# Decoder layer on one core: the PSUM bank of a score tile by its number in the whole walk, not within its pair of heads

## The reference, cut to what matters

```
q = concat([q_nope, rope(q_rope)]);  k = concat([k_nope, rope(k_rope)])
scores = einsum('blhd,bmhd->bhlm', q, k) / sqrt(DN + DR)
scores = where(tril, scores, -1e30)
attn = softmax(scores, axis=-1)
out = einsum('bhlm,bmhd->blhd', attn, v)
return out.reshape(B, L, H * DV) @ w_o
```

## Time and profile before

| | us |
|---|---|
| median of 3 runs | 1344.37 (1344.04 to 1345.14) |
| profiled execution, its own time | 1342.33 |
| its span, first to last instruction | 1340.50 |
| mean granted TensorE clock | 0.901 of full speed |
| attention walk, first to last score tile | about 165 to 928 |

### The profile page before, as it was taken

The page is one execution under the profiler, slowest core; times in us unless marked ns, Lnnn a source line. Parts: engine busy times, 40 slices in busy tenths (PEclk is TensorE's granted clock), DMA queues, the critical chain, the costliest instruction groups (busy, mean ns, idle before and its releaser), DMA issues.

```text
span 1340.5 us, 19020 instructions
## 1 busy us (share of the span) xinstructions
PE 1014.4 (76%) x6220; PEld 572.2 (43%) x6220; DVE 1043.0 (78%) x2856; ACT 678.5 (51%) x1451; POOL 273.0 (20%) x507
## 2 busy tenths in 40 slices
PE   1535488799989899989989999996834452547998
PEld 0323244445445445445445555553332331324564
DVE  5589677877887877887877888887189888886886
ACT  1539656656656656656656665654024221533443
POOL 1000112212212212212212221221021313122111
PEclk9759899899999989999989999999975776767999
DMA  9100022332332342322343333345271010000001
GB/s 358 69 1 1 1 50 49 68 58 50 68 61 50 67 115 52 67 58 50 68 112 58 60 69 64 91 97 154 71 220 47 17 32 0 0 1 8 35 38 48
DMA packets 200433, 86.59 MB, mean 65 GB/s; under 512 B 174600, under 2 KB 185864, under 8 KB 199824
## 3 DMA queue, kind: packets, MB, share of 16 engines
q1 hardware_dynamic: 200336, 85.38, 26.4%
HBM read 36.06 MB, written 7.34 MB: 32 GB/s over the span
## 4 chain that ended last, share of the span: by engine, by line
DVE 39%; PE 30%; ACT 12%; issue 10%; POOL 8%; DMA 1%; SPq 1%; DVEq 0%; ACTq 0%; POOLq 0%
PE bank L1765 5%; PE bank L889 4%; DVE arena L1471 4%; ACT arena L1204 4%; DVE arena L1447 4%; PE bank L1663 4%; DVE arena L1464 4%; POOL arena L1029 3%; ACT arena L1192 3%; POOL arena L1035 3%; PE bank L904 2%; DVE arena L648 2%; PE bank L1715 2%; DVE arena L644 2%; DVE arena L607 2%
## 5 line engine op out<-in xcount | busy, mean ns | idle before, releaser
L1174 ACT ACTIVATE arena<-bank,arena,scal 128x128 f32<-128x128 f32 (+3 forms) x256 | 158.1, 617 | 256.3 <-POOL arena L1024 253.8
L1765 PE MATMUL bank<-arena 128*128 128x512 f16 x768 | 186.0, 388 | 17.1 <-DVE arena L1477 12.8
L1447 DVE TENSOR_REDUCE arena<-bank 128x1 f32<-128x128 f32 (+3 forms) x256 | 124.0, 484 | 42.2 <-PE bank L1738 42.1
L1024 POOL TENSOR_TENSOR arena<-arena,scal 128x1 f32<-128x1 f32 x256 | 48.5, 190 | 529.2 <-DVE arena L1447 529.2
L1471 DVE SCALAR_TENSOR_TENSOR arena<-arena 128x128 f16<-128x128 f32 (+3 forms) x256 | 142.0, 555 | 9.1
L1464 DVE TENSOR_SCALAR arena<-arena 128x128 f16<-128x128 f32 (+3 forms) x256 | 140.9, 551 | 4.9
L1715 PE MATMUL bank<-arena 128*128 128x512 f16 x576 | 140.1, 390 | 0.0
L1750 PE MATMUL bank<-arena 128*128 128x512 f16 (+3 forms) x768 | 118.2, 305 | 19.6 <-DMA arena<-arena 19.4
L1765 PEld LDWEIGHTS bank<-arena 128*128 128x128 f16 x768 | 72.9, 99 | 99.9 <-DVE arena L1477 14.8
L1733 PE MATMUL bank<-arena 128*128 128x128 f16 (+3 forms) x256 | 77.5, 303 | 33.0 <-ACT arena L1174 25.2
L1482 DVE TENSOR_TENSOR arena<-bank,arena 128x512 f16<-128x512 f32 x64 | 43.9, 686 | 70.4 <-ACT arena L1183 70.4
(11 more groups left out here) (211 smaller groups left out, 2091.7 us busy)
## 6 DMA issues: line engine op xcount, KB each, us to landing
arena<-in_L_attn_w_qb SPq DMA_DIRECT2D x1, 4608.0 KB, 20.7
arena<-in_x SPq DMA_DIRECT2D x4, 1024.0 KB, 5.6
arena<-in_L_attn_w_o SPq DMA_DIRECT2D x1, 4096.0 KB, 31.0
arena<-arena SPq DMA_TRANSPOSE x256, 2.8
arena<-in_fside_BxS2xS SPq DMA_DIRECT2D x4, 1024.0 KB, 5.5
arena<-in_L_ffn_w SPq DMA_DIRECT2D x8, 512.0 KB, 7.8
out<-arena SPq DMA_DIRECT2D x16, 256.0 KB, 2.0
arena<-in_x SPq DMA_DIRECT2D x12, 256.0 KB, 3.1
```

Source lines behind the costliest of these rows:

```text
L1174: act.activation(pf(k), banks[S_BANKS[g % 3]][:, 0:n], ACT.Exp, bias=NB[:, k:k + 1], scale=sc_exp, accum_out=SUM[:, k:k + 1]).then_inc(s_e ...
L1447: dve.tensor_reduce(NEGM[:, (g & 3):(g & 3) + 1], banks[S_BANKS[g % 3]][:, 0:n], AX.X, ALU.max, negate=True).then_inc(s_max, 1)
L1765: last = pe.matmul(banks[Y_BANK][:, :], ot(gp, a, k, (q & 3) * P, P), wo(b, gp * GH + k), start=(k == 0 and n == 0), stop=(k == GH - 1 and ...
```

## The change

A tile's bank becomes S_BANKS[G % 3], on TensorE, VectorE and ScalarE alike, so that the rotation goes on from pair to pair. TensorE's wait becomes s_exp >= G - 2 for each tile from the fourth on: every tile takes the bank of the tile three before. For tile 0 of a pair that is the old tile 5, for tile 1 the old tile 6, for tile 2 the old tile 7. Nothing else is changed.

```diff
@@ exps (ScalarE)
-                act.activation(pf(k), banks[S_BANKS[g % 3]][:, 0:n], ACT.Exp, bias=NB[:, k:k + 1], scale=sc_exp,
+                act.activation(pf(k), banks[S_BANKS[G % 3]][:, 0:n], ACT.Exp, bias=NB[:, k:k + 1], scale=sc_exp,
                                accum_out=SUM[:, k:k + 1]).then_inc(s_exp, 1)
@@ row_max (VectorE)
-                dve.tensor_reduce(NEGM[:, (g & 3):(g & 3) + 1], banks[S_BANKS[g % 3]][:, 0:n], AX.X, ALU.max,
+                dve.tensor_reduce(NEGM[:, (g & 3):(g & 3) + 1], banks[S_BANKS[G % 3]][:, 0:n], AX.X, ALU.max,
                                   negate=True).then_inc(s_max, 1)
@@ scores (TensorE)
-                h, k, bp = g >> 2, g & 3, (i >> 3) & 1
-                n, bank = (k + 1) * P, banks[S_BANKS[g % 3]]
+                h, k, bp, G = g >> 2, g & 3, (i >> 3) & 1, 8 * i + g
+                n, bank = (k + 1) * P, banks[S_BANKS[G % 3]]
...
-                if not (i == 0 and g < 3):
-                    pe.wait_ge(s_exp, 8 * i + (g - 2 if g >= 3 else (-1, 0, -2)[g]))
+                if G >= 3:
+                    pe.wait_ge(s_exp, G - 2)
```

## The result

The changed kernel is slower: median 1349.05 us (8 runs, 1347.06 to 1351.47) against 1345.16 us of the kernel before (8 runs), ratio 1.0029 [1.0017, 1.0041]. That is +3.9 us, where +2.1 was forecast; it lies 0.25 us above the range. A second measurement, made beside the last experiments, gave 1349.06 (5 runs) against 1343.98 (21 runs), ratio 1.0042 [1.0028, 1.0055]. The profiled execution took 1347.66 us (span 1345.8), 5.3 us more than that of before.

A forecast was written before the change was run, and what follows sets the result against it. No engine was seen as full; VectorE's gapless queue mostly set the pace. Clock cost +2.4 and chain gain -0.3 gave +2.1 us, from 1342.33 to 1344.4 us, range 1343.3 to 1348.8.

The forecast's parts named there:

- Its mechanism and its sign: Merged TensorE idling in pairs 2 and 4 lowers the clock on chain work; slower by 2.1 us in sum.
- The gain on the chain: Tile 1 of pairs 25, 27 and 29 starts earlier, worth 0.1 us each on the chain, 0.3 us together.
- Tile 0: At a pair's start it still waits for qn_lo; idling shrinks about 0.06 us, bounds 0 and 0.12.
- Most of the 25.2 us are gone: TensorE's score matmul waits for the exp, 25.2 us in 20 waits, would mostly vanish from the profile.
- Tile 2: Its tighter wait, for the exp of old tile 7, costs 0; 2.4 us are left in pair 19.
- The clock in pairs 2 and 4: Clock falls in 4.6 us of merged idling, slowing prep_t to tile 3: 1.18 us each, bounds 0 and 4.76.
- its rival on the slow side: Slow clock in pairs 2 and 4 covers all of prep_mm: +4 to +6 us, 1348.4 to 1350.4; chance 0.27.
- the all-of-prep_mm case: In pairs 2 and 4 prep_mm goes from 3.10 to 6.2 us, each pair losing 2 to 3 us; chance 0.27.
- The steady blocks: In steady odd pairs TensorE gets 0.2 to 0.5 us ahead; clock cost taken as 0, bounds 0 and 1.2 us.

The follow-up runs named there:

- 4, 9 or 14 matmuls in pairs 2 and 4 alone: Changed kernel with that many unread matmuls before prep_t in pairs 2 and 4: 1345.14 and 1344.61 us with 4, 1342.55 with 9, 1342.74 with 14.
- filling: Kernel before, with 5 unread matmuls in TensorE's idle time before prep_t (even pairs 6 to 22) and before project (pairs 4 to 20): 1338.81 us.
- the two with old waits: Changed kernel with old waits at tiles 0 and 1 of each pair, 1345.54 us; or at tile 1 of pairs 2 and 4 only, 1344.80 us.

## Why the prediction was wrong

Its mechanism and its sign were right; the sizes of two terms were not.

- **The gain on the chain** (0.3 us): right in kind and near in size. The exp's step at pair 25 left the chain, VectorE's queue took its place, and pairs 25 to 30 gave 0.54 us.
- **Tile 0** keeps its wait, 2.30 us at 211.20 against 2.45 before, held by qn_lo: right, with 0.15 us gone where the bound was 0.12. "Most of the 25.2 us are gone" was wrong: 14.7 stay under the exp's name. They are not waits for it. At the start of pair 2 qn_lo ended at 211.14 (210.45 + 0.69), tile 0 began at 211.20, and the exp of the old tile 6, which it no longer waits for, ended at 211.21 (211.02 + 0.19):

```profile
210.45 0.69 DVE L1482 TENSOR_TENSOR arena<-bank,arena 128x512 f16<-128x512 f32 x1 [2.56 <-ACT arena L1183]
211.02 0.19 ACT L1174 ACTIVATION_READ_ACCUMULATOR arena<-bank,arena,scal 128x1 f32 x1
```

- **Tile 2** costs nothing: right, as the two traces of the changed kernel show.
- **The clock in pairs 2 and 4** (1.18 us each): this is the first step that failed. It was read from a block in which the clock fell 0.8 us after prep_t had begun. Here it fell before prep_t, and the slow stretch was 6.8 us, not 3.4, so prep_t and tile 2 paid too: 1.61 and 1.59 us in one trace, 1.94 and 1.75 in the other. The prediction had this as its rival on the slow side and gave the all-of-prep_mm case 2 to 3 us a pair; the truth lies between, and the slow clock covered prep_t and tile 2 but not all of prep_mm. Against that rival stood "such a stretch lasted 3.4 us here". The trace of the kernel before had a longer one, in pair 4, which the prediction took as pair 2's twin: 0.50 from 262.38 to 269.21 us, 6.8 us, begun in the idling before tile 1. It shows in nope_mm, which took 4.01 us there and 2.11 at the full clock:

```profile
264.22 0.39 PE L1733 MATMUL bank<-arena 128*128 128x256 f16 x1 [1.91 <-ACT arena L1174]
...
265.36 4.01 PE L1715 MATMUL bank<-arena 128*128 128x512 f16 x9
```

- **The steady blocks** (taken as 0, bounds 0 and 1.2 us): the second. Both traces of the changed kernel have falls in three blocks (at 373, 575 and 677 us in the first) where that of before has two (470 and 672): from pair 8 to pair 21 they take 2.4 and 2.5 us longer. One block more costs 2.1 us in the table above, not 1.2, since the fall in project came with it. The idling before prep_t also grew by 0.3 us to 2.60, but that it brings the third block is not shown: four traces with 4, 9 or 14 matmuls in pairs 2 and 4 alone idle 2.59 to 2.62 us there too and have two by pair 21. Over many runs this term is not resolved by itself; it is the rest of +3.9 to +5.1 us after 3.2 to 3.7 from pairs 2 and 4 and -0.5 from the late pairs: some 1 to 2 us.

The prediction also left out what the kernel before pays for such falls itself: filling takes 7.0 us off it (1345.82 to 1338.81).

## What to carry to other kernels

Before removing a wait of TensorE, ask what it will wait for next. If that is work of another engine that doesn't come sooner, the two idle times become one, and the price here was the clock: a slow stretch that had lain on matmuls nobody waits for moves onto the chain. Where such an idle time can't be removed, matmuls without a use, few enough to end before the releaser, can hold the clock; and a gain should be checked by what the filled version of the kernel before does.

## What was not expected of the hardware

- On prep_t and prep_mm of pair 2 the clock stayed at 0.50 for 6.8 us after 4.80 us of idling. The stretch began within the idling, so 2.6 us of it held no work, and still it did not end sooner. It was no single case: in pairs 2 and 4 of all thirteen traces the eight slow stretches that began in the middle of an idle time lasted 6.8 us, the fourteen that began at its end or on running matmuls 3.4 us.
- The two kinds of traces don't mix. From prep_t to tile 3 of pairs 2 and 4 it took 4.68 to 4.69 us in the seven traces of the kernel before, of the two with old waits and of the four with 14 matmuls, and 4.88 and 4.69 in that of the filled kernel before; it took 5.94 to 6.63 us in all five traces of the change with 0, 4 or 9 matmuls.
- 28 matmuls in pairs 2 and 4 and 5 each in 14 other places raised the mean granted clock only from 0.901 to 0.913, and took 0.45% off the time: the mean says little of which matmuls run slow. The filling's room can shrink: in each of the four traces with 14 matmuls the clock had fallen after tile 0's idling in one of pairs 2 and 4, nope_mm before the filling took 3.04 to 3.79 us in place of 2.11, and the filling ended only 0.1 us before prep_t began.
